# Local attention layers: probabilities divided on GpSimd, values stationary, split operands in the first feed-forward matrix

## The reference

```python
x = x + layernorm(causal_attention(layernorm(x)))   # 16 heads of 8, 4 groups
x = x + layernorm(local_layers(layernorm(x)))       # two layers, below
# one layer of local_layers, heads = 8, head size 64, window 64:
h = shift_token(x)
q, k, v = split(h @ wqkv)                           # 128 -> 3 x 512
q = l2norm(q) * qs;  k = l2norm(k) * ksc
q, k = rotary_xpos(q, k)
sim = 8 * q @ k.T            # each window of 64 against itself and the one before
attn = softmax(where(mask, -max, sim))
x = x + (attn @ v) @ wo
h = layernorm(shift_token(x)) * lg + lb
a, g = split(h @ w1 + b1)                           # 128 -> 2 x 341
x = x + (a * gelu(g)) @ w2 + b2
```

## Time and profile before

| what | value |
|---|---|
| three executions, median (lowest to highest) | 2219.2 us (2218.24 to 2221.23) |
| profiled execution, its own time | 2221.09 us |
| its span, first to last instruction | 2219.4 us |
| TensorE busy | 2010.5 us, 91% of the span |
| VectorE busy | 1806.2 us, 81% |
| ScalarE busy | 1623.4 us, 73% |
| GpSimd busy | 1380.4 us, 62% |
| TensorE clock granted, mean | 0.959 of 2.4 GHz |

### The profile page before, as it was taken

How to read it: one execution, slowest core, us unless ns; L and a number is a source line. 1 busy time by engine, 2 the same in 40 slices (tenths; PEclk the granted TensorE clock), 3 DMA queues, 4 the chain that set the end, 5 groups by cost and what they waited for, 6 DMA issues and landing times. The chain is left out here.

```text
span 2219.4 us, 52419 instructions
## 1 busy us (share of the span) xinstructions
PE 2010.5 (91%) x20476; PEld 1350.0 (61%) x20476; DVE 1806.2 (81%) x3455; ACT 1623.4 (73%) x3312; POOL 1380.4 (62%) x2090
## 2 busy tenths in 40 slices
PE   2999999999995489999999999999999999999971
PEld 1566666666663366676676676666666666666641
DVE  1788988888883468889989889896998998998746
ACT  1577777777774368888888888786878888888745
POOL 3598888888875665556556556554655655665403
PEclk9899999999998589999999999999999999999985
DMA  1001010010100111100100100111010011011014
GB/s 42 1 16 30 16 30 16 16 30 16 30 11 10 42 33 33 35 19 19 36 19 19 36 19 19 30 38 29 19 32 22 19 30 24 19 28 26 19 39 114
DMA packets 50548, 59.92 MB, mean 27 GB/s; under 512 B 8145, under 2 KB 43393, under 8 KB 48257
## 3 DMA queue, kind: packets, MB, share of 16 engines
q1 hardware_dynamic: 50304, 56.58, 10.2%
HBM read 17.90 MB, written 8.39 MB: 12 GB/s over the span
## 5 line engine op out<-in xcount | busy, mean ns | idle before, releaser
L982 POOL TENSOR_TENSOR b_part_b<-b_raw,b_tabs 128x256 f32<-128x256 f32 x512 | 432.3, 876 | 297.3 <-ACT b_raw L1041 262.7
L991 POOL TENSOR_TENSOR b_qk<-b_qk,b_part_b 128x1024 f32<-128x1024 f32 x128 | 332.2, 2596 | 271.1 <-DVE b_qk L1141 263.9
L1141 DVE TENSOR_TENSOR b_qk<-b_raw,b_tabs 128x512 f32<-128x512 f32 x256 | 296.7, 1199 | 0.1
L1242 PE MATMUL b_work<-b_w_high,b_h_high 128*128 128x512 f32 x384 | 191.1, 498 | 30.6 <-DVE b_h_low L1131 19.2
L473 POOL TENSOR_SCALAR_AFFINE_SELECT a_probs<-a_probs 128x256 f32<-128x256 f32 x512 | 203.3, 409 | 0.0
L1316 PEld LDWEIGHTS b_work<-b_v_even,b_pT 128*64 128x64 f32 x2048 | 136.9, 138 | 78.1 <-issue 72.6
L584 DVE TENSOR_REDUCE a_qpack<-a_pa 128x2 f32<-128x1024 f32 (+2 forms) x128 | 143.7, 1122 | 44.0 <-PE a_pa L655 41.4
L1062 ACT ACTIVATE b_probs<-b_sb,b_neg_max 128x128 f32<-128x128 f32 x512 | 147.9, 383 | 41.4 <-DVE b_neg_max L1163 41.0
L422 POOL TENSOR_TENSOR a_idle<-a_idle 128x1 f32<-128x1 f32 x432 | 86.6, 200 | 146.9 <-ACT a_probs L516 85.2
L1030 ACT ACTIVATE b_sq<-b_work 128x1024 f32<-128x1024 f32 x128 | 131.7, 1029 | 54.4 <-PE b_work L1244 43.7
L1068 ACT COPY b_pT<-b_work 128x512 f32<-128x512 f32 x256 | 154.4, 603 | 23.0 <-PE b_work L1306 23.0
(11 more groups left out here) (211 smaller groups left out, 5518.1 us busy)
## 6 DMA issues: line engine op xcount, KB each, us to landing
b_v_even<-b_v SPq DMA_DIRECT2D x32, 528.0 KB, 4.4
b_v_even<-b_v SPq DMA_DIRECT2D x32, 396.0 KB, 5.8
a_x_in<-in_L_attn_x SPq DMA_DIRECT2D x16, 256.0 KB, 3.2
a_x_again<-in_L_attn_x SPq DMA_DIRECT2D x16, 256.0 KB, 3.5
x_scratch<-a_x SPq DMA_DIRECT2D x16, 256.0 KB, 2.5
out<-c_y SPq DMA_DIRECT2D x4, 1024.0 KB, 5.4
b_w_raw<-in_L_ffn_wqkv SPq DMA_DIRECT2D x2, 768.0 KB, 4.3
b_tabs<-tab SPq DMA_DIRECT2D x2, 512.0 KB, 4.2
```

Source lines behind the costliest of these rows:

```text
L982: last = pool.tensor_tensor(part_b[:, x, :].rearrange("p (h d) -> p h d", d=DH)[:, :, lo:lo + DH // 2], raw[:, i % 2, x, :].rearrange("p ( ...
L991: pool.tensor_tensor(qk[:, i], qk[:, i], part_b[:], ALU.add).then_inc(c_made, 1)
L1141: last = dve.tensor_tensor(qk[:, i, x, :].rearrange("p (h d) -> p h d", d=DH), raw[:, i % 2, x, :].rearrange("p (h d) -> p h d", d=DH), ta ...
L1242: pe.matmul(x, h_high[:, t], w_high[:, cols], start=True, stop=False)
```

## The change

The probabilities are divided before they are turned. VectorE sums the rows of a pair's exponentials in SBUF and takes the reciprocals (sums); GpSimd multiplies the probabilities by them (norm), and p_turn waits for that. In values the head's values are now stationary and the turned probabilities stream, for a pair of heads at a time; the output comes out turned, so that divide and o_turn go, and copy_o reads the bank of values. The columns of ones go with them. The queries are no longer scaled by their inverse length: turn_q waits for rope_add alone, scale handles the keys, the row maxima are multiplied by the inverse lengths in a second small instruction, and the exponential takes the inverse length as its scale per partition. rope_cos reads queries and keys from their PSUM banks, and it frees them instead of the copies to raw; rope_sin waits for a semaphore of the copies. The first feed-forward matrix is split into a rounded part and a rest (w1_high, w1_low, padded with zeros to 3 x 128 columns), h2 likewise (h2_high by ScalarE, h2_low by VectorE), and each of its six products becomes three products of split operands (hidden3). h2 itself lies in the last third of hid. The shift of the values has one semaphore per buffer, h on GpSimd waits for the last projection to be filled and not for it to be read, and ORDER is a new list of 151 tasks for 153.

```diff
-VW = DH + 2
 SEQS = DEPTH * B
-OWN_STEPS = {"newton": 3, "divide": 1, "variance": 2, "rstd": 3, "weights_ffn": 1}
+OWN_STEPS = {"newton": 3, "row_max": 1, "sums": 1, "variance": 2, "rstd": 3, "weights_ffn": 1}
...
+    (0, "h", 0), (1, "copy_k", 1), (0, "low", 0), (2, "copy_p", 4), (2, "p_turn", 5, "w0"), (2, "sums", 3),
+    (2, "copy_p", 5), (1, "turn_k", 2, "x"), (1, "turn_k", 3, "o"), (1, "copy_k", 2), (0, "project_k", 0, "w1"),
+    (1, "copy_k", 3), (0, "project_q", 0, "w0"), (2, "norm", 6), (0, "square", 0), (0, "raw_q", 0),
+    (1, "scores", 0, "sa"), (2, "norm", 7), (1, "scores", 1, "sb"), (1, "row_max", 0), (0, "raw_k", 0),
+    (0, "rope_cos", 0), (1, "exp", 0), (1, "exp", 1), (2, "values", 1, "o"), (0, "rope_sin", 0), (2, "copy_o", 1),
+    (2, "p_turn", 6, "x"), (0, "rope_add", 0), (0, "square_sums", 0), (0, "project_q", 1, "w0"), (2, "copy_p", 6),
...
-        w1c = sb("w1c", [D, 2, HC * P])
+        w1_high, w1_low = sb("w1_high", [D, 2, HC * P], F32R), sb("w1_low", [D, 2, HC * P], F32R)
...
+        rs = sb("rs", [P, 2, TT, 2, HEADS])
...
-        v = sb("v", [P, 2, TT, HEADS, VW])
-        v_even = sb("v_even", [P, 2, TT, HEADS, VW])
+        v = sb("v", [P, 2, TT, HEADS, DH])
+        v_even = sb("v_even", [P, 2, TT, HEADS, DH])
+        raw_max = sb("raw_max", [P, PAIRS, 2, TT])
         neg_max = sb("neg_max", [P, 2, HEADS, TT])
...
-        h2 = sb("h2", [D, T])
+        h2_high, h2_low = sb("h2_high", [D, T], F32R), sb("h2_low", [D, T], F32R)
...
+        h2 = hid[:, HC - 1, :]
...
-                until_read(pool, "project_k", i, l, b)
+                pool.wait_ge(raw_made, n + 1)
...
+            def norm(l, b, h, slot):
+                pool.wait_ge(den_made, seq(l, b) * PAIRS + h // 2 + 1)
+                pool.tensor_tensor(probs[:, h % 4], probs[:, h % 4],
+                                   rden[:, h, :].rearrange("p (i a) -> p i a", a=1).to_broadcast([P, TT, P]), ALU.mult).then_inc(normed, 1)
...
-                    act.copy(w1c[:, half, 0:HID], bank_of[which][:, 0:HID]).then_inc(freed[which], 1)
+                    act.copy(w1_high[:, half, 0:HID], bank_of[which][:, 0:HID]).then_inc(w1_rounded, 1)
...
-                wait(act, a_made, n - 1)
                 wait(act, b_made, n - 1)
-                x, read = to_read(act, "project_q", i, l, b)
-                act.copy(raw[:, i % 2, 0, :], x).then_inc(read, 1)
+                x, _ = to_read(act, "project_q", i, l, b)
+                act.copy(raw[:, i % 2, 0, :], x)
 
             def raw_k(l, b, i, slot):
-                x, read = to_read(act, "project_k", i, l, b)
-                act.copy(raw[:, i % 2, 1, :], x).then_inc(read, 1)
+                x, _ = to_read(act, "project_k", i, l, b)
...
-                                          bias=neg_max[:, slot, h, i:i + 1])
-                last.then_inc(freed[which] if a else exp_made, 1)
+                                          bias=neg_max[:, slot, h, i:i + 1], scale=rs[:, slot, i, 0, h:h + 1])
+                if a:
...
+            def h2_high_(l, b, arg, slot):
+                until_read(act, "rstd_turn", 0, l, b)
+                act.copy(h2_high[:], h2).then_inc(h2_rounded, 1)
...
+                for half in range(2):
+                    dve.wait_ge(w1_rounded, 2 * l + half + 1)
+                    dve.tensor_tensor(w1_low[:, half, 0:HID], x[:, 0:HID], w1_high[:, half, 0:HID].bitcast(F32),
+                                      ALU.subtract).then_inc(freed[which], 1)
...
-                until_read(dve, "project_k", i, l, b)
-                for x in range(2):
-                    last = dve.tensor_tensor(qk[:, i, x, :].rearrange("p (h d) -> p h d", d=DH),
-                                             raw[:, i % 2, x, :].rearrange("p (h d) -> p h d", d=DH),
-                                             tabs[:, i, 0, x, :].rearrange("p (a d) -> p a d", a=1).to_broadcast([P, HEADS, DH]), ALU.mult)
-                last.then_inc(a_made, 1)
+                dve.wait_ge(raw_made, seq(l, b) * TT + i + 1)
+                for x, name in enumerate(("project_q", "project_k")):
+                    from_bank, read = to_read(dve, name, i, l, b)
+                    dve.tensor_tensor(qk[:, i, x, :].rearrange("p (h d) -> p h d", d=DH),
+                                      from_bank.rearrange("p (h d) -> p h d", d=DH),
+                                      tabs[:, i, 0, x, :].rearrange("p (a d) -> p a d", a=1).to_broadcast([P, HEADS, DH]),
+                                      ALU.mult).then_inc(read, 1)
...
-                a = qk[:, i].rearrange("p x (h d) -> p (x h) d", d=DH)
-                dve.tensor_tensor(a, a, rs[:, i * 16:(i + 1) * 16].rearrange("p (h a) -> p h a", a=1).to_broadcast([P, 16, DH]),
+                a = qk[:, i, 1].rearrange("p (h d) -> p h d", d=DH)
+                dve.tensor_tensor(a, a, rs[:, slot, i, 1, :].rearrange("p (h a) -> p h a", a=1).to_broadcast([P, HEADS, DH]),
                                   ALU.mult).then_inc(scaled, 1)
 
             def row_max(l, b, p, slot):
                 which, before = bank("scores", p, l, b)
                 dve.wait_ge(filled[which], before + 1)
-                dve.tensor_reduce(neg_max[:, slot, 2 * p:2 * p + 2, :], bank_of[which][:].rearrange("p a (i k) -> p a i k", i=TT),
-                                  AX, ALU.max, negate=True).then_inc(maxed, 1)
-
-            def divide(l, b, h, slot):
-                step = steps("divide", h, l, b)
-                x, read = to_read(dve, "values", h, l, b)
-                heads = x[:, 0:TT * VW].rearrange("p (i d) -> p i d", i=TT)
-                step(dve.reciprocal(rden[:, h, :], heads[:, :, DH]))
-                dve.tensor_tensor(o_norm[:, h // 2 % 2, :, h % 2, :], heads[:, :, 0:DH],
-                                  rden[:, h, :].rearrange("p (i a) -> p i a", a=1).to_broadcast([P, TT, DH]), ALU.mult).then_inc(read, 1)
+                step = steps("row_max", p, l, b)
+                step(dve.tensor_reduce(raw_max[:, p], bank_of[which][:].rearrange("p a (i k) -> p a i k", i=TT), AX, ALU.max, negate=True))
+                dve.tensor_tensor(neg_max[:, slot, 2 * p:2 * p + 2, :], raw_max[:, p],
+                                  rs[:, slot, :, 0, 2 * p:2 * p + 2].rearrange("p i a -> p a i"), ALU.mult).then_inc(maxed, 1)
+
+            def sums(l, b, p, slot):
+                step = steps("sums", p, l, b)
+                until_read(dve, "scores", p, l, b)
+                two = slice(2 * p % 4, 2 * p % 4 + 2)
+                step(dve.tensor_reduce(den[:, p], probs[:, two], AX, ALU.add))
+                dve.reciprocal(rden[:, 2 * p:2 * p + 2, :], den[:, p]).then_inc(den_made, 1)
...
+            def h2_low_(l, b, arg, slot):
+                dve.wait_ge(h2_rounded, seq(l, b) + 1)
+                dve.tensor_tensor(h2_low[:], h2, h2_high[:].bitcast(F32), ALU.subtract).then_inc(h2_split, 1)
...
-                pe.wait_ge(scaled, seq(l, b) * TT + i + 1)
+                pe.wait_ge(c_made, seq(l, b) * TT + i + 1)
                 x, full = to_fill(pe, "turn_q", i, l, b)
                 turned(x, full, i, 0)
 
             def turn_k(l, b, i, slot):
+                pe.wait_ge(scaled, seq(l, b) * TT + i + 1)
                 x, full = to_fill(pe, "turn_k", i, l, b)
...
             def p_turn(l, b, h, slot):
-                p, a = divmod(h, 2)
-                if a:
-                    x, full = to_fill(pe, "p_turn", h, l, b, after=("scores", p))
-                else:
-                    pe.wait_ge(exp_made, seq(l, b) * PAIRS + p + 1)
-                    x, full = to_fill(pe, "p_turn", h, l, b)
+                pe.wait_ge(normed, seq(l, b) * HEADS + h + 1)
+                x, full = to_fill(pe, "p_turn", h, l, b)
                 for i in range(TT):
                     last = pe.transpose(x[:, i * P:(i + 1) * P], probs[:, h % 4, i, :], ident[:])
                 last.then_inc(full, 1)
 
-            def values(l, b, h, slot):
-                if h == 0:
-                    pe.wait_ge(v_shifted, (seq(l, b) + 1) * 32)
-                x, full = to_fill(pe, "values", h, l, b, after=("p_turn", h))
+            def values(l, b, p, slot):
+                if p == 0:
+                    pe.wait_ge(v_shifted[slot], (seq(l, b) // 2 + 1) * 32)
+                for a in range(2):
+                    until_read(pe, "p_turn", 2 * p + a, l, b)
+                x, full = to_fill(pe, "values", p, l, b)
                 for w in range(WINS):
-                    i = w // 2
-                    values_ = (v if w % 2 else v_even)[:, slot, i, h, :]
-                    last = pe.matmul(x[half_rows(w), i * VW:(i + 1) * VW], pT[:, h % 4, w * WIN:(w + 1) * WIN], values_,
-                                     start=True, stop=True)
-                last.then_inc(full, 1)
-
-            def o_turn(l, b, p, slot):
-                x, full = to_fill(pe, "o_turn", p, l, b, after=("values", 2 * p + 1))
-                for i in range(TT):
```

(24 more changed lines are left out.)

104 lines of the change are left out of this document (45 added, 59 removed).

## The result

The changed kernel takes 2230.5 us, the median of 11 runs (2223.3 to 2240.7), against 2218.5 (2217.7 to 2221.2) before: a ratio of 1.0052 with a 95% interval of 1.0041 to 1.0064. It is 0.5% slower, where 2163 was forecast. Its profiled execution took 2235.3 us, with a span of 2233.5.

A forecast was written before the change was run, and what follows sets the result against it. TensorE bounds the 41.70 us interval; its work falls to 37.8, plus 0.9 and 1.1 of waits gives 39.8. Over 26 regular intervals 49 us go, elsewhere 7: 2163 us, range 2120 to 2225 (own range 2145 to 2185).

The forecast's parts named there:

- four small products behind the row maxima, 0.7: VectorE, per sequence: the added small products were priced at 0.7 us together, within 15.0 us of added work.
- six instructions still read two operands in SBUF: VectorE: four scalings and two low parts may stand until GpSimd's instruction ends; 0.5 us each, 3 us per sequence.
- an allowance for handovers: Regular interval: TensorE and ScalarE, at the same height, wait for one another; 1.1 us more, beside 0.9 idle.
- the 2.0 us given for TensorE's waits: Regular interval: 0.9 and 1.1 us added to TensorE's 37.8 us of work, giving 39.8 us.
- Rival 2: ScalarE becomes the bound and keeps its waits, as before exponentials for the row maximum: interval 43.2, 2269 us; chance 0.12.
- Rival 3: Banks w0 and w1: VectorE's cosine pair behind the row maximum holds projections, 3.0 us; interval near 41.7, 2216 us; chance 0.10.
- Rival 1: ScalarE stays covered and TensorE alone sets the pace: interval 38.7 us, 3.0 less, 2130 us; chance 0.20.

## Why the prediction was wrong

- **TensorE: right.** 38.07 us busy, and 37.22 where it isn't held up, against 37.8. A pair of heads in the values takes 1.08 us, three products of the feed-forward 0.70 to 0.80 from start to start:

```profile
1059.38 0.34 PE L1333 MATMUL b_work<-b_pT,b_v_even 128*64 128x64 f32 x4
...
1060.46 0.50 PE L1362 MATMUL b_work<-b_h_high,b_w_high 128*128 128x512 f32 x1
...
1061.26 0.39 PE L1362 MATMUL b_work<-b_h_high,b_w_high 128*128 128x512 f32 x1
...
1061.96 0.40 PE L1362 MATMUL b_work<-b_h_high,b_w_high 128*128 128x512 f32 x1
```

- **ScalarE: right.** 36.92 us against 37.7. The exponentials come 0.344 us apart (eight in 2.75), so that the second operand costs 0.09, as taken from the last stage:

```profile
1035.60 2.90 ACT L1065 ACTIVATE b_probs<-b_sa,b_neg_max,b_rs 128x128 f32<-128x128 f32 x8 [0.86 <-DVE b_neg_max L1178]
1038.35 0.62 ACT L1090 COPY b_oT<-b_work 128x512 f32<-128x512 f32 x1
```

- **VectorE's and GpSimd's large instructions: near or better.** Cosine products take 682 ns for 690, scalings 688 for 640, divisions 1044 for 1280; GpSimd is busy 29.3 us for 33.
- **The step that failed: "four small products behind the row maxima, 0.7", and the count "six instructions still read two operands in SBUF".** The four products read two operands in SBUF too; so do the layer norm's refining steps, and the variance step stands in the same way. The price of 0.17 us each was that of an instruction with GpSimd idle; the products took 128.9/32 = 4.0 us per sequence. The six that were counted lost next to nothing (means of 688 and 692 ns), because GpSimd was not running: of their 192 starts only four, all before 805 us, met a GpSimd instruction. The small ones, left uncounted for their size, met one nearly every time and took up to 2.4 us each. I had the rule from the earlier trace rows, and applied it by the size of VectorE's work, while its price is what is left of GpSimd's instruction.
- **A second error lies in the sum: busy times and an allowance for handovers.** VectorE's total was not far off (37.2 for 36), and still the interval was 1.9 us longer than forecast, because the small steps stand where TensorE waits for their end. Without them it is 38.60, below the 39.8 forecast: the 2.0 us given for TensorE's waits were too much for the rest (1.4 there) and lacked the ones that decided. The forecast missed by 68 us: 56 is what its sum took off for the shorter interval, and the other 12, mostly slips, were not in the prediction at all.
- **The rivals.** Rival 2 falls: ScalarE waits 0.9 us per sequence for the row maximum, not over 2, and shorter exponentials took 0.2 us off the interval. It came nearest, as it named the second instruction behind the row maxima, but priced it as a wait of ScalarE and not of TensorE at the feed-forward product behind it in VectorE's queue. Rival 3 falls: no wait of TensorE for the cosine products shows in the 7 sequences above; that its interval near 41.7 came true is luck. Rival 1's 38.7 us is what the kernel without the small steps does, but not the changed kernel, and its condition, exponentials at their old price, did not hold. None of them had the mechanism.
- That both kernels run at 41.70 is a coincidence, as the intervals from 38.15 to 41.75 show. What stays open is the regular interval of the kernel with constant scales: there the variance step is longer by 0.4 us, which does not explain the 1.3 us that are missing to the expectation.

The Trainium skill ("SBUF — State Buffer", section "SBUF: two separate sides") says that of a GpSimd instruction and a VectorE instruction with two SBUF inputs (if GpSimd's reads SBUF), or in a two-port mode, whichever starts first has an exclusive lock for its whole length, and the other blocks fully. The traces agree for the products, 1.27 us behind a half and 2.36 behind a whole rope_add; nothing in the rule exempts an instruction on 4 elements. Whether the variance step, with one SBUF operand and a constant, runs in such a mode no run here shows; it stands all the same.

## What to carry to other kernels

Where GpSimd is busy, count every VectorE instruction with two SBUF operands, also those on a few elements, and steps such as the variance's; price each at the length of GpSimd's longest instruction if it stands on the path. Remove all of them from the path at once: of the three kinds here the two taken out alone gave 0.4 us each at most, and all three together 3.1, because the next one takes over the wait. And put what TensorE waits for ahead of such an instruction in the queue, not behind it: that alone took 1.1 us off the interval.

## What the hardware showed unexpectedly

- Between two GpSimd instructions without a gap VectorE sometimes comes in and sometimes not. The variance step that began at 1261.48, 0.5 us ahead of a division's end, stood through rope_add as well; in the regular interval it began as far ahead of a division's end and finished with it (0.54 us). The changed kernel's runs spread over 17 us, those of the kernel before over 4; that the slips make this spread is likely, but was not tested.
- Not every small instruction stands. VectorE's reciprocals on the same 8 elements, with one operand, never did, though 29 of the 128 began while a GpSimd instruction ran (the other times it was idle):

```profile
L1186 DVE RECIPROCAL b_rden<-b_den x128: 202/203/205, 780.1 to 2136.7; 128x8 f32<-128x8 f32 x128
```
